# Sixteen landing semaphores for all indirect transfers of a graph network kernel, one transfer under way on each

## What is computed

```
edge_index = stack([src, dst])
x = layernorm(x + segment_max(relu([x[dst], x[src]-x[dst]] @ W1 + b1) @ W2 + b2, dst))   # 0 where a node has no edge
agg = segment_sum(x[src], dst)
x = layernorm(x + relu((x + agg) @ V1 + c1) @ V2 + c2 + x @ Vres + cres)
```

## Time and profile before

| what | value |
|---|---|
| median of 3 runs | 1256.63 us (1256.03 to 1257.38) |
| profiled execution, span from first to last instruction | 1254.0 us |
| median less span: what lies around the span | 2.63 us |
| PE, DVE, ACT, POOL busy in the span | 87%, 75%, 71%, 61% |
| mean granted PE clock, share of full speed | 0.948 |
| indirect transfers on POOL | 784 |

### The profile page before, as it was taken

One profiled execution on the slowest core, in us unless ns is written; L12 is line 12 of the kernel. 1 busy time (PEld: TensorE's weight loads), 2 busy tenths in 40 slices (PEclk: granted clock), 3 DMA queues, 4 the chain that ended last, 5 costly groups with the idle time before them and its releaser, 6 DMA issues.

```text
span 1254.0 us, 27368 instructions
## 1 busy us (share of the span) xinstructions
PE 1086.1 (87%) x7463; PEld 838.8 (67%) x7463; DVE 935.2 (75%) x3648; ACT 895.2 (71%) x3876; POOL 765.8 (61%) x798
## 2 busy tenths in 40 slices
PE   5699999995199999999889999999999999999500
PEld 3577777773166666666568888888887888888400
DVE  6588888875088888888868777777777999999300
ACT  2688878774078888788778888888888777777400
POOL 5666666666656666566346666666666566656666
PEclk9799999998599999999999999999999999999855
DMA  4587877764167777677676666666664666666311
GB/s 132 171 228 226 235 228 228 233 191 115 54 188 212 214 208 225 200 212 206 186 211 190 192 191 194 193 197 195 195 195 149 201 204 205 208 210 198 107 39 38
DMA packets 172195, 232.05 MB, mean 185 GB/s; under 512 B 25508, under 2 KB 90641, under 8 KB 172044
## 3 DMA queue, kind: packets, MB, share of 16 engines
q1 hardware_dynamic: 145372, 180.84, 46.3%
q0 software_dynamic: 25088, 48.94, 15.2%
q10 hardware_dynamic: 1584, 0.53, 0.2%
HBM read 129.48 MB, written 102.96 MB: 185 GB/s over the span
## 4 chain that ended last, share of the span: by engine, by line
PE 43%; issue 19%; DMA 17%; POOL 15%; DVE 4%; ACT 1%; POOLq 0%; SPq 0%; DVEq 0%; ACTq 0%
PE psY L1104 8%; PE psY L1103 8%; PE psH L1112 8%; DMA edge_rows<-in_x,idx 8%; POOL edge_rows L502 8%; PE psT L1096 4%; PE psE L1104 3%; PE psE L1103 3%; PE psE L1259 3%; DMA xd_early<-in_x,idx 3%; PE psE L1096 3%; POOL xd_early L502 3%; DMA out<-edge_rows,idx 3%; POOL out L509 3%; POOL src_bc L502 2%
## 5 line engine op out<-in xcount | busy, mean ns | idle before, releaser
L1103 PE MATMUL psY<-wc,hT 128*128 128x128 f32 x1568 | 307.1, 278 | 2.9 <-ACT o_rows L954 2.5
L1104 PE MATMUL psY<-wcr,xT 128*128 128x128 f32 x1568 | 306.5, 278 | 0.0
L502 POOL DMA_INDIRECT edge_rows<-x1e_table,idx x196 | 193.1, 985 | 134.6 <-DMA edge_rows<-x1e_table,idx 75.2
L509 POOL DMA_INDIRECT out<-edge_rows,idx x196 | 193.1, 985 | 120.8 <-DMA out<-edge_rows,idx 70.6
L502 POOL DMA_INDIRECT edge_rows<-in_x,idx x196 | 188.2, 960 | 114.9 <-DMA edge_rows<-in_x,idx 76.5
L929 ACT ACTIVATE junk<-psY 128x128 f32<-128x128 f32 x784 | 208.6, 299 | 50.9 <-PE psY L1104 50.1
L1103 PEld LDWEIGHTS psY<-wc,hT 128*128 128x128 f32 x1568 | 241.9, 195 | 4.2 <-issue 4.2
L1104 PEld LDWEIGHTS psY<-wcr,xT 128*128 128x128 f32 x1568 | 241.6, 195 | 0.0
L592 DVE TENSOR_SCALAR x<-x_in,mv,rs 128x128 f32<-128x128 f32 x784 | 222.5, 356 | 0.5
L1112 PE MATMUL psH<-xT,wc 128*128 128x512 f32 x392 | 205.2, 605 | 15.2 <-issue 9.0
L929 ACT ACTIVATION_READ_ACCUMULATOR junk<-psY 128x1 f32 x784 | 179.7, 231 | 0.0
(11 more groups left out here) (125 smaller groups left out, 2017.4 us busy)
## 6 DMA issues: line engine op xcount, KB each, us to landing
x_in<-in_x SPq DMA_DIRECT2D x196, 256.0 KB
out<-o_rows SPq DMA_DIRECT2D x196, 256.0 KB
src_bc<-src_dram SPq DMA_DIRECT2D x49, 256.0 KB, 4.6
mask<-mask_dram SPq DMA_DIRECT2D x98, 128.0 KB, 4.4
x1eT_spill<-x1eT SPq DMA_DIRECT2D x49, 256.0 KB
x1e_table<-edge_rows SPq DMA_DIRECT2D x49, 256.0 KB, 3.1
x1e_table<-shared SPq DMA_DIRECT2D x49, 256.0 KB, 3.7
x1eT<-x1eT_spill SPq DMA_DIRECT2D x49, 256.0 KB, 2.9
```

The lines of the kernel that those rows point to most:

```text
L502: nc.gpsimd.indirect_dma_start(to, None, table, bass.IndirectOffsetOnAxis(idx[:, what, t:t + 1], 0), **kw).then_inc(done, 16)
L509: nc.gpsimd.indirect_dma_start(table, bass.IndirectOffsetOnAxis(idx[:, SCAT, t:t + 1], 0), frm, None, bounds_check=limit, oob_is_err=False ...
L1103: t_.matmul(to[:, cut(t)], h[:, cut(t)], wc2[:, :], start=t == 0, stop=False, skip_group_check=True)
L1104: last = t_.matmul(to[:, cut(t)], xt[:, cut(t)], wcr[:, :], start=False, stop=t == TILES - 1, skip_group_check=True)
```

## The change

The 20 landing semaphores of the four kinds go. All 784 transfers get a running number in the order in which POOL issues them (`src_number` and its sisters), transfer n counts on semaphore `landed[n % 16]`, and before POOL issues transfer n it waits until transfer n - 16 has landed. The readers wait tile by tile: PE before each transpose of a gathered tile, DVE four times ahead of `xs_stats`. Pairs and pauses stay as they are.

```
+    FLIGHT = 16
+    EARLY = GROUPS // 2 + 1
...
+        landed = sems("indirect_landed", FLIGHT)
...
+        def src_number(g):
+            return TILES * (g + (SLOTS if g >= EARLY else 0))
+        def dst_number(g):
+            return TILES * (g + (EARLY if g < SLOTS else GROUPS))
+        def z_number(g):
+            return TILES * (2 * GROUPS + g)
+        def scatter_number(g):
+            return TILES * (3 * GROUPS + g)
+        def await_landing(eng, n):
+            eng.wait_ge(landed[n % FLIGHT], 16 * (n // FLIGHT + 1))
...
-            def gather(to, table, what, t, done, every):
+            def gather(to, table, what, t, n):
+                if n >= FLIGHT:
+                    await_landing(pool, n - FLIGHT)
                 nc.gpsimd.indirect_dma_start(to, None, table, bass.IndirectOffsetOnAxis(idx[:, what, t:t + 1], 0),
-                                             **kw).then_inc(done, 16)
+                                             **paired(n)).then_inc(landed[n % FLIGHT], 16)
+                pause(n)
...
             def gather_src(g):
-                j, r = divmod(g, SLOTS)
-                wait(pool, src_gathered[r], 16 * TILES * j)
...
-            for r in range(SLOTS):
-                pool.wait_ge(final[r], 16 * TILES * len(range(r, GROUPS, SLOTS)))
+            for n in range(scatter_number(GROUPS) - FLIGHT, scatter_number(GROUPS)):
+                await_landing(pool, n)
...
             def xs_stats(g):
-                    dve.wait_ge(src_gathered[g % SLOTS], 16 * TILES * (g // SLOTS + 1))
+                    for t in range(TILES):
+                        await_landing(dve, src_number(g) + t)
...
-            def transpose4(to, rows, done=None):
+            def transpose4(to, rows, done=None, number=None):
                 for t in range(TILES):
+                    if number is not None:
+                        await_landing(pe, number + t)
                     last = t_.transpose(to[:, cut(t)], rows[:, cut(t)], ident[:, :])
```

## The result

The changed kernel takes 1260.29 us (median of 7 runs, 1259.53 to 1262.52) against 1257.38 us for the kernel before, run on the same chip (7 runs, 1256.03 to 1258.94): a ratio of 1.0028, 95% interval 1.0018 to 1.0039. That is slower by 0.28%, some 3 to 3.5 us (the medians are 2.9 us apart). The forecast was 1256.0 us and no difference that can be told; the time lies in the range given (1253.5 to 1264.0), but the kernel is slower by more than the noise, and that was not forecast.

What follows compares the result with a forecast made beforehand. POOL bounds to 340 us, stage A's steps to 637, POOL to 1254. Span 1254.0 less 0.3, less 0.7, plus 0.4, with 2.63 us around it, gives 1256.0 us, no tellable difference; 8-in-10 range 1253.5 to 1264.

Steps and rivals of the forecast that it cites:

- the first rival: POOL, second of a pair: the added wait lies in the open, 0.06 us over 352 pairs, 21 us slower; chance 0.14.
- the sum: Span 1254.0 us, less 0.3 (stage A), less 0.7 (counted scatter heads), plus 0.4 (other heads): 1253.4 us.
- the cover that the prediction read from the earlier trace: POOL, between the two of a pair: work hides under the first's 0.98 us write, so an added wait costs 0.
- the third (PE's load ahead): PE, gathered transposes: waits between them stop the load ahead, 0.29 us each, 78 us at most; chance 0.02.
- the second has nothing for it: Rival on POOL's writes: moved phases leave them less disturbed, a third of 13 us spared, 4 us faster; chance 0.08.
- POOL's third stretch: From 636.61 us to the end: POOL never without work, 392 transfers, setting the end at 1254 us.
- the gaps fixed in size: POOL's table gathers and scatters: gaps between transfers taken as constant, with 6.2 us put down to dense stores.
- the first stretch's count: POOL, 10 to 332.7 us: 203.2 us busy plus pair gaps of 0.30 and 0.81 us make 321 of 322.7 us.
- no idle time but its own dispatch and pauses: POOL's first stretch, 212 transfers from 10 to 332.7 us: no other idle time, 321 of 322.7 us accounted for.
- The predicted table gather start: POOL's table gathers after the change were to start at about 636.3 us, against 636.61 before.
- the 0.3 us less that I gave stage A: PE at 516.81 us: three transposes already done when it waits for the last tile, so stage A ends 0.3 us earlier.
- the 2.63 us around the span: Time outside the profiled span, added to the 1253.4 us span to give the forecast of 1256.0 us.

Runs made afterwards that it cites:

- the two runs made for them: Kernel before plus a satisfied wait on every second of a pair: ratio 0.9994; changed kernel with PE waiting once a group: ratio 1.0028 to before.
- A shift by two: Changed kernel (16 semaphores) with two no-ops at the start of POOL's list: 1258.35 us, ratio 1.0013 to the kernel before.
- its second trace: The kernel before, unchanged, run and profiled again: 1257.28 us in one run.

## Why the prediction was wrong, point by point

**What was right.** That the time lies in the stated range is luck: the upper end was there for the first rival, which didn't come. No transfer waits for a landing 16 back: behind a pause the profile names the pause's own release, and group heads kept their gaps, apart from the few that the sum priced; with 64 semaphores the profile has landings for every kind, 2.7 to 4.1 us in the median. The second of a pair kept 0.30 us, apart from the long gaps and the three at count loads. There the cover that the prediction read from the earlier trace rows has an end: in before the load of 0.29 us, at 1167.9 us, starts 0.2 us ahead of the first one's write and left the gap at 0.30; in after a load of 0.68 us, at 1171.7 us and as early beside its write, left 0.45. The counted scatter heads went from 1.18 to 1.11 us, as the sum had it (0.06 each). After, the row with [0.45] is one of the three at a count load, the next is a counted head, the last a plain head:

```profile
1173.37 0.98 POOL L526 DMA_INDIRECT out<-edge_rows,idx  x1 [0.45 <-issue]
1175.47 0.98 POOL L526 DMA_INDIRECT out<-edge_rows,idx  x1 [1.11 <-issue]
1176.75 0.98 POOL L526 DMA_INDIRECT out<-edge_rows,idx  x1 [0.30 <-issue]
...
1181.69 0.98 POOL L526 DMA_INDIRECT out<-edge_rows,idx  x1 [0.88 <-DMA out<-edge_rows,idx]
```

PE's transposes with three more waits still start 0.44 us a group of four, with the loads back to back. The loads of the target rows start at 511.51 us, while by the profile the transposes of the source rows run from 511.18 to 511.78 us, so the loads still go ahead:

```profile
511.07 0.47 PEld L1108 LDWEIGHTS psE<-ident,edge_rows 128*128 128x128 f32 x4
511.51 0.47 PEld L1108 LDWEIGHTS psE<-ident,src_bc 128*128 128x128 f32 x4
511.94 0.30 PEld L1222 LDWEIGHTS psE<-ehT,raw 128*128 128x128 f32 x2
```

So the first rival (the wait in the open) and the third (PE's load ahead) are out, by these rows and by the two runs made for them; the second has nothing for it, the means of a write are 987, 984 and 960 ns where they were 985, 985 and 960. DVE's four waits stayed hidden: its wait for PE's transposes right behind is still 0.49 us a step (21.6 us over 44 from 340 to 640 us).

**The step that failed** is the reading of POOL's third stretch, "the gaps fixed in size", and with it the first stretch's count of "no idle time but its own dispatch and pauses". From that I costed the change only by the waits that it adds and moves. The gaps are not fixed: seven of some 1.1 to 2.0 us and a few of 0.3 us over the usual stood in the trace of before, 9.5 us of long ones, under the releaser "issue" that I took for dispatch. The rows at hand already say it. The sum of the first stretch leaves 1.8 us of 322.7 over: 1.39 of them are the long gap at 113, 0.40 the small one at 30. And the "issue" part of the table gathers is 33.5 us, where 98 seconds of a pair at 0.30 us are 29.4: the two long gaps there add 2.5, and the small gap at 428, 1.09 us, counts there whole. The change has two effects on them that I didn't cost:

- *The long gaps follow the landing semaphores.* With 16 semaphores in turn they come every 98 transfers at 1.9 us: 11.8 us against 9.5. One moved from transfer 229, in stage A, to 211, in the stretch that POOL sets. With 64 semaphores the same numbering has 7.2 us and loses nothing to before. This is shown by the runs with 8, 16, 32 and 64, and by the two with 4 and 16 semaphores in which POOL waits for the same landings at the same heads (104 and 98 apart).
- *One instruction more shifts the list.* In after, waits that need an instruction of their own, the first of them at the first early target gather (0.87 us there), put more of the places 68 + 128k on firsts of a pair: four more on the path, 1.3 us. A shift by two takes them away, and some 2 us in the median with them.

The predicted table gather start, 636.3 us, was missed by 2.1 us, all of it in the first stretch of this pair of executions (before has 638.23 us in its second trace); the 0.3 us less that I gave stage A is no more than the 0.25 us seen there, too small to be called shown. Of the 4.1 us by which POOL ends later in the profiled execution, 3.3 us are the moved and lengthened long gaps that lie on its path (1.83 + 1.5), 1.3 the small ones (0.31 + 0.95), 0.4 the three at count loads, which belong to the execution; of the 3.3 us, 0.57 are there because a long gap met a count load; 0.6 to 0.7 come off at the counted heads and 0.25 in stage A.

One term of the sum was mis-sized beside that: the 2.63 us around the span. In every run with both figures on record, the time is 1.7 to 1.9 us above the span (1259.93 and 1258.1 for after), so by my estimate the profiled execution of before took some 1255.8 us, and the other 0.8 us is its distance from the median.

**What stays open.** What POOL does in a long gap, for no trace shows it. Why the long gaps of the kernel before stand 116, 96, 88, 92, 104 and 92 apart: its 20 semaphores are used kind by kind, four transfers on each, and I have no rule that gives these places. By the law of one transfer a semaphore none could be over 113 apart. The lengths give a hint: by the line above those of before stand for 88, 84, 88, 63, 103 and 80 transfers, and the next long gap comes 28, 12, 0, 29, 1 and 12 transfers later than that; by the line, my estimate, the start of a pair's second would come no later than the ordinary 1.24 us for up to some 28 transfers. No run tests this. Nor does the law give the 104 of four semaphores for four transfers each. In the runs with 8, 16, 32 and 64 the reach of POOL's waits grew with the number of semaphores; 64 semaphores with waits 16 back would part the two, and weren't tried, nor were more than 64.

## What to carry to other kernels

Where one engine issues hundreds of like instructions and sets the end, list the gap before each of them, not the mean or a sample: a few long gaps without a releaser may recur at fixed places. Here a change of semaphores moved the long ones, and a change of the instruction count the small ones. Ask of such a gap what it is periodic in, and change that number alone. A satisfied wait cost nothing here as long as it rode on the instruction (0.30 us with and without); one that needed an instruction of its own behind a pause cost 0.06 us or more.

## What the runs showed of the hardware

- In every run here the indirect transfers on POOL have a long gap first at the 114th, then every 113 - (F - 1) with F landing semaphores in turn, one transfer under way on each (F of 8, 16, 32, 64: 106, 98, 82, 50 apart; typically 2.1, 1.9, 1.55 and 0.8 us where 0.31 is usual). POOL's waits for them can stand at the group heads without moving it (98 apart).
- A first of a pair at place 68 + 128k of POOL's list in these traces starts about 0.3 us later (1.11 for 0.81); a second of a pair at such a place, behind the write of the first, does not (0.30 to 0.32).
- Two more waiting instructions behind the pause cost about 0.15 us a group head (0.96 against 0.81); the same waits spread over the transfers, one each, left the gaps at 0.81 and 0.30.
- Loading a count from SBUF into a register on POOL between the two transfers of a pair hid under the write of the first when it took 0.28 to 0.30 us (gap 0.30 in the changed kernel) and did not when it took 0.68 or 0.69 us (0.43 to 0.45).
